# Delta stage: copies, the layer norm's application and the gate's scaling move from VectorE to ScalarE

## The reference

```python
attn = jnp.where(strict, -(kb @ sw(k)), 0.0)          # chunks of 32 tokens, 4 heads of 64
T = jnp.linalg.inv(jnp.eye(chunk) - attn)
u = T @ v
w = T @ kb
def step(S, inp):                                     # scan over chunks
    q_i, k_i, u0, w_i = inp
    local = jnp.where(incl, q_i @ sw(k_i), 0.0)
    u_i = u0 - w_i @ S
    o_i = q_i @ S + local @ u_i
    return (S + sw(k_i) @ u_i, o_i)
...
paths = jnp.stack([fir_s(v), fir_m(v), fir_l(v), delta_path, v], axis=3)
stats_flat = jnp.concatenate([_stats(paths[..., p, :]) for p in range(P)], -1)
logits = jax.nn.gelu(concatenate([hs, stats_flat]) @ gW1 + gb1) @ gW2 + gb2
tau = jax.nn.softplus(log_tau) + 0.5
probs = jax.nn.softmax(logits / tau[:, None], -1)
eps = jax.nn.sigmoid(eps_logit) * 0.2
probs = probs * (1.0 - jnp.sum(eps, -1, keepdims=True)) + eps
o = jnp.einsum('blhp,blhpd->blhd', probs, paths)
o = o * rsqrt(mean(o * o, -1) + 1e-05) * norm_w
x = _layernorm(x + o @ Wo)
```

## Time and profile before

| | us |
|---|---|
| median of 3 runs | 998.28 |
| lowest, highest run | 990.76, 999.94 |
| span of the profiled execution | 1000.6 |
| TensorE matmuls busy | 883.4 (88%) |
| VectorE busy | 632.2 (63%) |
| ScalarE busy | 431.9 (43%) |
| GpSimd busy | 343.5 (34%) |

### The profile page before, as it was taken

The page is one execution under the profiler, slowest core; times in us unless marked ns, Lnnn a source line. Parts: engine busy times, 40 slices in busy tenths (PEclk is TensorE's granted clock), DMA queues, the critical chain, the costliest instruction groups (busy, mean ns, idle before and its releaser), DMA issues.

```text
span 1000.6 us, 18366 instructions
## 1 busy us (share of the span) xinstructions
PE 883.4 (88%) x6859; PEld 660.2 (66%) x6859; DVE 632.2 (63%) x1488; ACT 431.9 (43%) x781; POOL 343.5 (34%) x318
## 2 busy tenths in 40 slices
PE   7799788779889898889889998979997999999995
PEld 5576566657667675668656555555785777777774
DVE  5799797667898888752656778774553343333255
ACT  5688565335545544433134444445331322222221
POOL 9322201022555455620201223223631142222584
PEclk9899999868997977999989999999998999999998
DMA  5699679996454323212895112000402222221421
GB/s 167 193 273 282 192 174 242 294 225 144 100 112 74 81 49 74 62 49 90 325 388 188 51 56 85 23 23 25 155 10 89 60 64 64 60 62 55 148 65 63
DMA packets 144631, 123.54 MB, mean 123 GB/s; under 512 B 89952, under 2 KB 126752, under 8 KB 143264
## 3 DMA queue, kind: packets, MB, share of 16 engines
q1 hardware_dynamic: 141136, 112.99, 40.1%
q0 software_dynamic: 3408, 9.38, 2.5%
HBM read 74.05 MB, written 48.29 MB: 122 GB/s over the span
## 4 chain that ended last, share of the span: by engine, by line
PE 62%; DVE 16%; POOL 7%; ACT 6%; issue 4%; DMA 3%; SPq 1%; POOLq 0%; DVEq 0%; ACTq 0%
PE ps L2507 9%; PE ps L1913 6%; PE ps L2522 5%; DVE cross_room L1946 3%; PE ps L2371 3%; PE ps L1348 3%; PE ps L1853 3%; PE ps L666 3%; PE ps L2384 2%; POOL hank L345 2%; PE ps L1975 2%; PE ps L1614 2%; POOL kept L2654 2%; PE ps L423 2%; PE ps L1356 2%
## 5 line engine op out<-in xcount | busy, mean ns | idle before, releaser
L1991 ACT ACTIVATE cross_room<-ps 128x1024 f32<-128x1024 f32 x64 | 65.5, 1024 | 98.1 <-PE ps L1917 98.1
L1946 DVE TENSOR_REDUCE cross_room<-ps 128x4 f32<-128x1024 f32 x64 | 78.0, 1223 | 38.8 <-PE ps L1913 38.0
L2507 PE MATMUL ps<-wr,xbT 128*128 x312 | 100.6, 465 | 1.8 <-ACT xbT L2543 1.8
L1913 PE MATMUL ps<-kept,cross_room 32*128 32x256 f32 x512 | 73.3, 407 | 21.8 <-DVE cross_room L1946 18.8
L2596 POOL DMA_INDIRECT y_dram<-yb,dest_row x39 | 37.6, 963 | 136.2 <-DVE dest_row L2572 132.0
L1316 POOL TENSOR_TENSOR st<-st,exponent 128x20 f32<-128x20 f32 x16 | 56.6, 3535 | 69.1 <-DVE st L1291 67.8
L2507 PEld LDWEIGHTS ps<-wr,xbT 128*128 128x128 f32 x312 | 59.3, 191 | 30.1 <-issue 3.5
L1917 PE MATMUL ps<-cross_room,kept 32*128 32x256 f32 x512 | 74.5, 409 | 0.0
L1913 PEld LDWEIGHTS ps<-kept,cross_room 32*128 32x128 f32 x512 | 46.7, 188 | 39.6 <-issue 19.1
L550 DVE SCALAR_TENSOR_TENSOR room<-room 128x256 f32<-128x256 f32 x144 | 58.3, 477 | 11.6 <-ACT room L499 11.6
L2581 DVE TENSOR_TENSOR cross_room<-cross_room,ps 128x352 f32<-128x352 f32 x39 | 20.3, 521 | 60.3 <-PE ps L2507 58.9
(11 more groups left out here) (349 smaller groups left out, 2261.1 us busy)
## 6 DMA issues: line engine op xcount, KB each, us to landing
xs_dram<-params SPq DMA_DIRECT2D x17, 1040.0 KB, 17.8
room<-in_gW SPq DMA_DIRECT2D x8, 1280.0 KB, 8.0
tok_dram<-room SPq DMA_DIRECT2D x8, 768.0 KB, 6.3
fir_dram<-room SPq DMA_DIRECT2D x6, 1024.0 KB, 7.2
paths<-fir_dram SPq DMA_DIRECT2D x48, 128.0 KB, 3.8
xb<-xs_dram SPq DMA_DIRECT2D x39, 130.0 KB, 2.4
hank<-rt_dram SPq DMA_DIRECT2D x8, 512.0 KB, 7.6
yr<-y_dram SPq DMA_DIRECT2D x16, 256.0 KB, 3.3
```

Of the source, the lines that this page charges most:

```text
L1913: m1 = nc.tensor.matmul(ps[:, c, t * T:(t + 1) * T], strips(qS[b % 3], g, c)[:, t * P:(t + 1) * P], kS(b, g)[c * CH:(c + 1) * CH], start=T ...
L1946: V.tensor_reduce(mx[:, :, g, XD + 2 * h * CH:XD + (2 * h + 1) * CH + 1:CH].rearrange("p t c -> p c t"), ps[:, pair(h), :].rearrange("p c ...
L1991: S.activation(pT[g % 2][:, pair(h)].rearrange("p c k t -> p (c k t)"), ps[:, pair(h), :].rearrange("p c n -> p (c n)"), ACT.Exp).then_inc ...
L2507: m = nc.tensor.matmul(ps[:, 2 * (j % 2) + half, 0:FF], xbT[j % 2][:, k, :], wr[:, bass.ds(e, 1), k, half, :].rearrange("p e n -> p (e n)" ...
```

## The change

Lines below are those of the new kernel where a + stands ahead.

- The copies of the values u as they come (L1254, L1265), of the state (L1261) and of the last triangle blocks (L1138) leave VectorE and are written on ScalarE: L1226, L1242, L1238 and L1107. The generator dve_states is gone. The last triangle blocks have a signal of their own (g2).
- The layer norm is applied on ScalarE (L1508) as y·rstd + (-mean·rstd). So GpSimd makes -mean·rstd too, with two more instructions on 128x2. L1508 stands four pieces behind the copy of the turned output.
- The gate's bias and 1/tau are applied to the turned logits (20 rows, one per head and path) in the copy that ScalarE makes of them anyway (L1374); VectorE's two instructions for it go, and its first reduce reads PSUM. The parameters for this are 20x1 columns; log_tau and gb2 are loaded in that form.

```diff
@@ act_small / dve_small @@
-        lt, t1, t2, env.itau, env.keep = small_views(0, 5, H)
+        lt, t1, t2, env.itau, env.gbt = (v[0:H * NPATH] for v in small_views(0, 5, 1))
+        env.keep = small_views(4 * H, 1, H)[0]
...
+            V.tensor_tensor(env.gbt, env.gbt, env.itau, ALU.mult).then_inc(*s.small.up())
@@ pe_invert, pe_states @@
-            pe.wait_ge(s.gw, 4 * b)
+            pe.wait_ge(s.g2, 2 * b)
...
-            pe.wait_ge(s.gw, 4 * b + 4)
+            pe.wait_ge(s.g2, 2 * b + 2)
@@ act_invert (from dve_invert) @@
+            act.wait_ge(s.gw2_made, b + 1)
+            for h, bank in enumerate((3, 0)):
+                S.copy(by_head(g0[b % 2][:])[HS[0], h, :, HS[1]],
+                       ps[HS[0], bank, 0:NP // HL * DH].rearrange("p (q j) -> p q j", j=DH)).then_inc(*s.g2.up())
@@ act_states (from dve_states, which is gone) @@
             yield
+            act.wait_ge(s.u0_made, b + 1)
+            act.wait_ge(s.u1_turned, b)
+            S.copy(flat(uT[:, 0]), ps[:, 4, 0:KT * P]).then_inc(*s.uT.up())
             act.wait_ge(s.w_made, b + 1)
...
+            act.wait_ge(s.s_made, b + 1)
+            act.wait_ge(s.cleared, 3)
+            for h in range(HL):
+                S.copy(sbd[HS[h], :, HS[h]],
+                       ps[HS[h], 5, 0:KT * P].rearrange("p (c n) -> p c n", c=KT)[:, :, HS[h]]).then_inc(*s.sbd.up())
+            yield
+            act.wait_ge(s.u1_made, b + 1)
+            S.copy(flat(uT[:, 1]), ps[:, 4, 0:KT * P]).then_inc(*s.uT.up())
             yield
@@ act_gate @@
-            S.copy(lgT[:], ps[0:H * NPATH, 6, 0:T]).then_inc(*s.lgT.up())
+            act.wait_ge(fir.small, SMALL)
+            S.activation(lgT[:], ps[0:H * NPATH, 6, 0:T], ACT.Identity, bias=env.gbt, scale=env.itau).then_inc(*s.lgT.up())
@@ dve_gate @@
             dve.wait_ge(s.lg_turned, b + 1)
-            dve.wait_ge(s.mix, 3 * b)
-            V.tensor_tensor(lg[:].rearrange("p t h n -> p t (h n)"), ps[:, 7, 0:TT * H * NPATH].rearrange("p (t n) -> p t n", t=TT),
-                            gb2[:].unsqueeze(1).broadcast_to([P, TT, H * NPATH]), ALU.add).then_inc(*s.gate_step.up())
-            dve.wait_ge(s.gate_step, k0 + 1)
-            V.tensor_tensor(lg[:], lg[:], per_head(itau[:]), ALU.mult).then_inc(*s.gate_step.up())
-            dve.wait_ge(s.gate_step, k0 + 2)
-            V.tensor_reduce(sm[:], lh, AX.X, ALU.max).then_inc(*s.gate_step.up())
-            dve.wait_ge(s.gate_step, k0 + 3)
-            V.tensor_tensor(lh, lh, sm[:].unsqueeze(2).broadcast_to([P, NP, NPATH]), ALU.subtract).then_inc(*s.gate_step.up())
+            V.tensor_reduce(sm[:], turned, AX.X, ALU.max).then_inc(*s.gate_step.up())
+            dve.wait_ge(s.gate_step, k0 + 1)
+            dve.wait_ge(s.mix, 3 * b)
+            V.tensor_tensor(lh, turned, sm[:].unsqueeze(2).broadcast_to([P, NP, NPATH]), ALU.subtract).then_inc(*s.gate_step.up())
@@ act_project_out (from dve_project_out) @@
+            for _ in range(4):
+                yield
+            act.wait_ge(s.rstd, 4 * b + 4)
+            for t in range(TT):
+                S.activation(y[b % 2][:, t, :], y[b % 2][:, t, :], ACT.Identity, bias=mv[:, t, 0:1],
+                             scale=mv[:, t, 1:2]).then_inc(*s.applied.up())
             yield
@@ dve_project_out @@
-            for _ in range(6):
-                yield
-            dve.wait_ge(s.rstd, 2 * b + 2)
-            for t in range(TT):
-                V.tensor_scalar(y[i][:, t, :], y[i][:, t, :], mv[:, t, 0:1], mv[:, t, 1:2], ALU.subtract,
-                                ALU.mult).then_inc(*s.applied.up())
@@ pool_project_out @@
             G.tensor_scalar(mv[:, :, 1], mv[:, :, 1], 1.0, 1e-5, ALU.mult, ALU.add).then_inc(*pool.tick(s.rstd))
-            pool.wait_ge(s.rstd, 2 * b + 1)
+            pool.in_turn()
+            G.tensor_scalar(mv[:, :, 0], mv[:, :, 0], -1.0, 0.0, ALU.mult, ALU.add).then_inc(*pool.tick(s.rstd))
+            pool.wait_ge(s.rstd, 4 * b + 1)
             pool.in_turn()
             G.tensor_tensor(mv[:, :, 1], mv[:, :, 1], env.exponent[:, 0, 0:TT], ALU.pow).then_inc(*pool.tick(s.rstd))
+            pool.wait_ge(s.rstd, 4 * b + 3)
+            pool.in_turn()
+            G.tensor_tensor(mv[:, :, 0], mv[:, :, 0], mv[:, :, 1], ALU.mult).then_inc(*pool.tick(s.rstd))
```

81 lines of the change are left out of this document (28 added, 53 removed).

## The result

The changed kernel takes 986.32 us (median of four runs, 982.72 to 989.73) against 998.26 of the kernel before: a ratio of 0.9885, with a 95% interval from 0.9843 to 0.9927. A second set of runs gave 985.02 (ratio 0.9877, 0.9826 to 0.9928). The forecast was 986.3, faster by over 1% with a chance of 0.54. The kernel is faster, by 1.15%; both intervals hold the limit of 1%, so on which side of it the change lies isn't settled. The profiled execution has a span of 987.9 us; forecast for it was 988.6.

A forecast was written before the change was run, and what follows sets the result against it. TensorE and VectorE were taken as nearly full, ScalarE as half empty. Gains and losses summed to 12.0 us, taking the profiled span from 1000.6 to 988.6; less 2.3 for the runs' median, 986.3. Range 979 to 995.

The forecast's parts named there:

- Full rounds: Rounds at full clock with gate and output parts: 28.5 us becomes 25.7, a gain of 2.8 us each.
- c: Between VectorE's products and sums in a round: the triangle copy leaves the gap, gaining 0.7 us.
- term a: Gate chain: VectorE's subtraction ends 2.1 us earlier, ScalarE's queue then sets the Exp, and L1211 starts 0.7 us earlier.
- Term b: VectorE's three products beside GpSimd's work: 1.5 us of overlap instead of 2.7, so 2.9 us instead of 3.87; gain 1.0.
- rival 2: GpSimd's instruction blocks VectorE's products; they gain 0.3 instead of 1.0 us in five rounds, total 990 us; chance 0.14.
- Doubtful rounds: Rounds from 294.25 and 352.12, with a lower-clock stretch: gains between 0.7 and 3.7 or 2.8 us, taken as 2.2 and 1.7.
- The tail: Round from 405.97: L1508 waits for rstd, L1348 comes 2.9 us later, other waits go; net -0.3 us.
- The end: Last round's square behind L1508 costs 0.2 us; last L1508 behind the key copies delays the engines' meeting by 1.6 us.
- The early wait: At 213.77 TensorE waits 2.40 us for VectorE's L1261; on ScalarE nothing is ahead of that copy: gain 2.4 us.
- 1: The lower clock stays and TensorE sets three rounds, 3 to 5 us less gain: 989 to 991 us; chance 0.16.
- 3: ScalarE's queue takes VectorE's place, moved copies waiting behind scalings and Gelu: 994.5 us; chance 0.12.
- 4: Slower: rstd comes late through long added GpSimd instructions, six rounds and the tail lose: about 1012 us; chance 0.06.

The follow-up runs named there:

- the kernel with both placings: Changed kernel with batch 5's norm pair moved behind the last gate's copies and the last two norms one group of four key copies earlier on ScalarE: 979.51 us, ratio 0.9836.

## Why the prediction was right, point by point

- **Full rounds (2.8).** Right, as a sum and by its terms: c alone is 0.67 in a run of its own (0.7 forecast), L1210 starts 0.7 earlier, products 2.88 (2.9), square to logits 0.45 (0.35). What the prediction lists as parts of term a, the copy of the values and the gate's two instructions, is very unequal: 1.15 and 0.2 alone. And a and b are not separate causes; undoing the values' copies alone brings the long products back. Of the 2.8 us the runs account for 2.3 part by part; the last 0.5 is open.
- **Term b's mechanism.** The size was right, 1.0, the mechanism was not. I had scaled the length by the time spent beside GpSimd. My own two rows, put on one line, would have given 2.7 for 1.5 us, and the time beside GpSimd was 1.13 in fact, so that the 2.9 I took was met is partly luck. In truth single instructions block each other, and it counts how many GpSimd instructions stand in the way of a product: two before, one after. This is rival 2's rule. No product ended before GpSimd did (T+14.06), and the last one ended 1.75 us behind that, within the "two or three of 0.68" that rival 2 has. Only its price was wrong: the 0.3 comes from counting three and from GpSimd's end at T+14.4; counted with two, its own sum gives the 1.0.
- **Doubtful rounds (2.2 and 1.7).** Too small: 3.7 and 3.4. They were tied to two particular rounds, while the second trace of the kernel before shows that the stretch at the lower clock wanders. In the round from 352.12 the lower clock (0.82) cost the kernel before hardly anything, 28.55 against 28.32 in its second trace (0.94 there), and so all of the gain came. That VectorE and not TensorE set the pace there would explain it; no run shows that. The error is 3.2 us to the good in the first trace.
- **The tail (-0.3).** The mis-sized term: -3.6 in the first traces, -0.75 in the second (23.26 against 22.51, at granted clocks of 0.93 and 0.92). The mechanism was named rightly, and L1348's delay of 2.9 measured as 3.3. It is there in all eight traces that keep the pair's place: in each L1508 waits 2.64 or 2.65 us for GpSimd. The step "Against it ... net -0.3" credited 2.6 us of other waits; they did go, but L1346 now waits 0.62 us for L1503 in their place ahead of the marker at 414.01, and 0.8 to 0.9 us are lost (23.26 against 22.38 and 22.51). The other 2.7 us of the first trace are the clock, which had no place in the sum. It fell ahead of the wait in both traces of the changed kernel; in the second it came back within the wait, in the first only at 404.6. Whether the wait keeps it down longer is not shown: the eight traces with the pair in its old place took 23.3 to 26.2 us, at 0.80 to 0.93, and the three with the pair moved 21.3 each, at 0.92.
- **The round from 380.67 (0.7).** 0.2 in the first traces, 1.1 in the second (26.07 against 24.98); the other kernels show 21.75 to 25.65 here. The clock sets it.
- **The end (-1.6 and -0.2).** The meeting cost 1.6, exactly as worked out. That the piece lost only 0.6 in all is the clock again and no gain of the change: behind its last marker the kernel before ran at the lower level in its first trace (row 1) and not in its second (row 2), which is 1.6 us shorter there. Against the second the end lost 2.2, which is 0.4 more than the forecast's 1.8.

```profile
428.35 3.34 PE L1356 MATMUL ps<-hid,gw 128*20 128x256 f32 x8
427.28 1.90 PE L1356 MATMUL ps<-hid,gw 128*20 128x256 f32 x8
```

- **The early wait (2.4).** It stood in TensorE's waits: 2.4 and 2.1 before, 1.9 with the copies put back, none after. The span can't confirm it.
- **Rivals.** 1 (the lower clock takes more) came true in the tail and, in the first traces, in the round ahead of it; 3 and 4 did not occur: in a full round TensorE waits 0.37 us for L1245, which stands behind a moved copy, and less for any moved copy itself, and rstd was there at T+9.8 with the norm starting at T+11.9.

Errors of +3.2, +1.2 and +1.2 on one side and -3.3, -0.5 and -1.0 on the other nearly cancel, and most of them are the clock's. From first marker to next stage the change gained 10.1 us in the first traces and 11.2 in the second, where the terms of the sum give 9.6. The hit to 0.1 us is luck; the range and the full round were not.

## What to carry to other kernels

Move work to the emptier engine where the queue it leaves feeds a chain (here two copies ahead of a softmax), and then look at every queue place the work arrives at: once for the steady round, and once for each round in which its neighbours are missing, since a wait that is covered in the middle stood bare in the tail. Ask of each moved part what it brings alone; one of the five, the norm, brought nothing in the full rounds, and where it was put it cost 4.2 to 7.0 us over the last two pieces against the kernel with both placings. Compare by intervals between markers where the span varies by more than the change is worth.
